# GpSimd copies the indices of a block of gathers two at a time, ahead of each pair, in a four-stage graph network on one core

## The chip, the cores and the metric

The program runs on one core of one Trainium2 chip. The metric is the device time of one execution in microseconds (us); lower is better. The engines are named as the profile names them: PE (TensorE), DVE (VectorE), ACT (ScalarE), POOL (GpSimd), and SP (SyncE), whose instructions are nearly all issues of transfers. "PEld" is PE's loading of weights. A "q" behind a name (SPq) is the engine's sequencer, which waits, computes registers and issues transfers.

## The reference

The graph has 6,250 nodes with 64 features and 200,000 edges sorted by their target. Four networks follow one another, each with a residual sum and a layer norm. The part around the change is the first one, two layers of graph attention with four heads:

```python
z = (x @ W).reshape(N, H, F)
el = jnp.sum(z * al, axis=-1)
er = jnp.sum(z * ar, axis=-1)
e = jax.nn.leaky_relu(el[src] + er[dst], 0.2)
m = jax.ops.segment_max(e, dst, num_segments=N)
ex = jnp.exp(e - m[dst])
s = jax.ops.segment_sum(ex, dst, num_segments=N)
alpha = ex / s[dst]
msg = z[src] * alpha[..., None]
out = jax.ops.segment_sum(msg, dst, num_segments=N) + b
```

What `el[src]` and `z[src]` ask for is one row of a table for each edge. The other three networks (a graph convolution of three layers, a plain sum over neighbours, and two convolutions with edge features) are sums over the same edges and come later in the program.

## The kernel before

**Blocks of gathers (POOL).** `table_d` in device memory holds, for each node, its features, a one and four logits (69 floats, 276 bytes). The 200,000 edges, padded to 98 x 2,048, are cut into 98 blocks. For a block, POOL issues 16 indirect DMAs (the gathers, L798), each of which brings 128 rows of the table into one of the three slots of a ring in SBUF; then it stores the slot to `msg_d` in device memory (L782), so that the rows lie there in the order of the edges. It does this for both attention layers (`blocks_pool`, called once for each), 196 blocks and 3,136 gathers in all. All indices of the core lie in `row_idx`; before the gathers of a block, POOL copies the block's 16 columns into `idx_cur` (L793) and waits on the semaphore `idx_here` for its own copy. The store of block j-1 is issued behind the third gather of block j (`store`), and behind the ninth POOL waits for that store to land and raises `msg_ready` (`ready`).

**Pace.** POOL doesn't gather as early as it can. DVE raises `dve_step` by eight for each group that it works through, in several portions. For each block a place was computed beforehand; ahead of the gathers k = 0, 2, 4, ... POOL waits until `dve_step` has reached that place plus k * 10 // 16. The first three blocks of the first layer have no place. The places are set so that a block is asked for 32 steps (four groups) ahead of the first group that reads it.

**Groups of windows.** A window is ten nodes and up to 384 edges, a group is five windows; there are 125 groups in each layer, five to a pass of a loop of 25. For a group, SP in program order:

- waits until DVE (and PE) are done with the slot, and loads the records of the next group's edges from `rec_d` (L498, five transfers) and, for two or three groups in five, their edge features (L500, five transfers);
- waits until `msg_ready` has reached the last block that the group needs, and until PE is done with the group of five groups ago (`win_psum`);
- loads `er_sl` (L516) and the five windows' rows from `msg_d` (L519).

DVE makes the one-hot matrices of three windows (first layer) or two (second layer) for the adjacency of the later networks (L1018, L1019), then works on the group's rows (first at L1041): logits, their maximum, the difference (L1045 to L1070, L1151). ACT scales one-hots (L1889), takes exponentials (L1949) and empties PE's banks; PE makes the adjacency products (L1610, L1612) and the weighted sums (L1631). SP can load a group's rows some groups before DVE works on them. After the second attention layer, the convolutions read the adjacency matrices back from device memory; POOL has no work there.

`wait_reg` (L354 to L356) is a wait on a register's value, which also raises a counter of its own.

Of the kernel before, what the change touches and what calls it, by code (L numbers as in the profile page):

```python
# [65 lines left out]
BK = 16  # L66
BLK = P * BK
NBLK = EP // BLK
# [5 lines left out]
PER_BLOCK = STEPS * NGR // NBLK  # L74
# [6 lines left out]
def build(nc, a):  # L81

    ctx = ExitStack()
    with ctx:
# [3 lines left out]
        def sem(name):  # L88
            return ctx.enter_context(nc.semaphore(name))
# [32 lines left out]
        def new(parts, *dims):  # L122
            off = top[0]
            top[0] += (int(np.prod(dims)) + 7) // 8 * 8
            return at(off, parts, *dims)
# [28 lines left out]
        row_idx = new(P, EC).bitcast(I32)  # L154
        idx_cur = new(P, RING, BK).bitcast(I32)
# [148 lines left out]
        def s(name):  # L304
            if name not in S:
                S[name] = sem(name)
            return S[name]
# [45 lines left out]
        def wait_reg(eng, semaphore, value):  # L353

            eng.wait_ge(semaphore, value)
            eng.sem_inc(s(f"passed_{'sp' if eng is nc.sync else 'pool'}"), 1)  # L356

        def rounds(eng, count, peel=True):

            if peel:  # L360
                yield 0
            with eng.Fori(int(peel), count) as i:
                yield i
# [8 lines left out]
        def range_from_one(eng, count):  # L372

            with eng.Fori(1, count) as i:
                yield i
# [39 lines left out]
        def first(b):  # L415
            return isinstance(b, int) and b == 0
# [358 lines left out]
        def blocks_pool(pool, layer):  # L775

            g_ = nc.gpsimd
            uses_before = [layer * len(range(i, NBLK, RING)) for i in range(RING)]

            def store(j, i, uses):  # L780
                wait_reg(pool, gathered[i], uses * (16 * BK) + 16 * BK)
                g_.dma_start(msg_d[bass.ds(j * BLK, BLK), :].rearrange("(p k) f -> p (k f)", k=BK), ring[:, i]).then_inc(msg_stored[i], 16)  # L782

            def ready(i, uses):
                wait_reg(pool, msg_stored[i], uses * 16 + 16)
                pool.sem_inc(s("msg_ready"), 1)

            def block(j, i, uses, former):
                if not isinstance(j, int) or j >= RING or layer:
                    place = pool.value_load(pace_row[0:1, layer, bass.ds(j, 1)], min_val=1, max_val=HEAD + 2 * NGR * STEPS + PER_BLOCK)  # L790
                else:
                    place = None
                g_.tensor_copy(idx_cur[:, i], row_idx[:, bass.ds(j * BK, BK)]).then_inc(s("idx_here"), 1)  # L793
                wait_reg(pool, s("idx_here"), j + (layer * NBLK + 1))
                for k in range(BK):
                    if place is not None and k % 2 == 0:
                        wait_reg(pool, s("dve_step"), place + k * PER_BLOCK // BK)
                    g_.indirect_dma_start(ring[:, i, k * XC:(k + 1) * XC], None, table_d, bass.IndirectOffsetOnAxis(  # L798
                        ap=idx_cur[:, i, k:k + 1], axis=0)).then_inc(gathered[i], 16)
                    if former is not None and k == BK // 8:  # L800
                        store(j - 1, (i - 1) % RING, former)
                    if former is not None and k == BK // 2:
                        ready((i - 1) % RING, former)

            def former_uses(it, i):
                return it + uses_before[(i - 1) % RING] - (1 if i == 0 else 0)

            pool.wait_ge(s("table_stored"), 16 * (layer + 1))
            if layer == 0:
                for i in range(RING):  # L810
                    block(i, i, 0, None if i == 0 else 0)
                pool.wait_ge(s("items_back"), 32)
            for it in (rounds(pool, NBLK // RING) if layer else range_from_one(pool, NBLK // RING)):
                for i in range(RING):
                    block(it * RING + i, i, it + uses_before[i], None if first(it) and i == 0 else former_uses(it, i))
            it = NBLK // RING
            for i in range(NBLK % RING):
                block(it * RING + i, i, it + uses_before[i], former_uses(it, i))
            last = NBLK - 1
            store(last, last % RING, last // RING + uses_before[last % RING])  # L820
            ready(last % RING, last // RING + uses_before[last % RING])
# [1292 lines left out]
```

## Time and profile before

| what | us |
|---|---|
| median of three runs (lowest, highest) | 7727.45 (7714.45, 7744.26) |
| the profiled execution, its own time | 7731.27 |
| span of the profile, first to last instruction | 7729.6 |
| POOL's first gather block to its last gather, first layer | 125.66 to 2753.6 |
| the same, second layer | 3027.59 to 5627.6 |
| busy: PE, DVE, ACT, POOL | 4457.3, 4150.8, 2129.1, 3270.2 |

The span is 1.7 us shorter than the profiled execution's own time. The program has three parts: the first attention layer up to about 2,860 us, the second up to about 5,860 us, the convolutions to the end. POOL works in the first two alone. Waits of SP are counted as SPq; its instructions are not counted as busy, so its load is read from how far apart its issues stand.

### The profile page before, as it was taken

Reading aid. Unit: us, or ns where it says so; the run is one execution under the profiler, and the core shown is the slowest. Engines: PE = TensorE matmul, PEld = TensorE weight load, DVE = VectorE, ACT = ScalarE, POOL = GpSimd, SP = SyncE. Lnnn points to the kernel's source line nnn. Section 1 sums busy time; section 2 is a strip of 40 time slices with the busy share of each in tenths; the row PEclk is TensorE's granted clock in tenths of the full one; section 3 lists DMA queues with packets and bytes.
Section 4 is the critical chain, followed back from the end, with each engine's and each line's share of the span. In section 5 each row is a group of like instructions: output and inputs, shape, how many; then the busy total and the mean of one; then the engine's idle time right before and its main releaser. Section 6 shows DMA issues by size and latency. Waiting matters only on the chain.

```text
span 7729.6 us, 118765 instructions
## 1 busy us (share of the span) xinstructions
PE 4457.3 (58%) x28553; PEld 2928.7 (38%) x28553; DVE 4150.8 (54%) x13273; ACT 2129.1 (28%) x5938; POOL 3270.2 (42%) x3549
## 2 busy tenths in 40 slices
PE   1455555555555565344444444444477988888865
PEld 1223333223233235122222222222256767676754
DVE  3566676767676663455655565556574111223344
ACT  0344444444444441133333233333320000000000
POOL 3666666656565612666666666656600000000000
PEclk9666766666776665566666666666667999999988
DMA  5454454545444532344444444444437989899976
GB/s 88 112 144 134 136 145 131 145 129 145 136 143 134 143 113 49 97 111 122 121 112 121 121 121 116 120 110 123 120 108 287 416 340 416 345 416 401 373 291 260
DMA packets 934339, 1390.68 MB, mean 180 GB/s; under 512 B 483496, under 2 KB 689474, under 8 KB 917769
## 3 DMA queue, kind: packets, MB, share of 16 engines
q1 hardware_dynamic: 687776, 912.42, 35.0%
q0 software_dynamic: 128976, 222.12, 11.6%
q10 hardware_dynamic: 117332, 253.47, 8.8%
q8 instruction: 71, 1.16, 0.1%
q14 instruction: 184, 1.51, 0.1%
HBM read 1014.16 MB, written 373.27 MB: 179 GB/s over the span
## 4 chain that ended last, share of the span: by engine, by line
issue 18%; SPq 16%; PE 14%; another core or an unknown queue 13%; DVE 13%; DMA 13%; ACT 7%; DVEq 4%; ACTq 2%
DMA arena<-adj_w_d 8%; ACT arena L1889 4%; DMA arena<-adj_c_d 4%; SPq L498 4%; SPq L519 4%; PE bank L1754 3%; PE bank L1755 2%; PE bank L1758 2%; SPq L485 2%; DVE arena L1018 2%; PE bank L1716 2%; SPq L500 2%; PE bank L1610 1%; DVE arena L1041 1%
## 5 line engine op out<-in xcount | busy, mean ns | idle before, releaser
L798 POOL DMA_INDIRECT arena<-table_d,arena x3136 | 3093.4, 986 | 1956.7 <-issue 974.0
L1610 PE MATMUL bank<-arena 128*128 128x500 f16 x3750 | 1351.9, 497 | 1312.4 <-issue 720.1
L1631 PE MATMUL bank<-arena 128*65 128x40 f32 x7500 | 649.0, 257 | 1053.8 <-ACT arena L1949 538.8
L1610 PEld LDWEIGHTS bank<-arena 128*128 128x128 f16 x3750 | 430.2, 122 | 2026.1 <-issue 1798.0
L1889 ACT ACTIVATE arena<-arena 128x128 f16<-128x128 f16 x3750 | 1126.6, 392 | 239.1 <-DVEq L1119 133.0
L1631 PEld LDWEIGHTS bank<-arena 128*65 128x65 f32 x7500 | 618.0, 171 | 1174.0 <-issue 611.6
L1754 PE MATMUL bank<-arena 125*128 125x250 f16 x3750 | 857.9, 274 | 156.2 <-DMA arena<-adj_w_d 132.9
L1018 DVE TENSOR_SCALAR arena<-arena 128x500 f16<-128x500 f16 x1875 | 681.7, 364 | 411.5 <-issue 207.2
L1755 PE MATMUL bank<-arena 125*128 125x250 f16 x3750 | 853.9, 273 | 0.0
L1612 PE MATMUL bank<-arena 128*128 128x500 f16 x1875 | 695.7, 474 | 203.6 <-issue 200.1
L1104 DVE SCALAR_TENSOR_TENSOR arena<-arena,bank 128x250 f16<-128x250 f16 x1250 | 455.8, 412 | 559.2 <-ACT arena L1913 297.8
L1910 ACT ACTIVATE arena<-bank 128x500 f16<-128x500 f32 x625 | 365.2, 584 | 1296.8 <-remote 641.3
L1932 ACT ACTIVATE arena<-bank 65x200 f32<-65x200 f32 x250 | 83.1, 333 | 1574.0 <-remote 1523.0
L1019 DVE TENSOR_SCALAR arena<-arena 128x128 f16<-128x128 f16 x1875 | 511.5, 273 | 0.0
L1758 PE MATMUL bank<-arena 125*128 125x250 f16 x3750 | 443.1, 274 | 98.0 <-DMA arena<-adj_c_d 91.9
L1041 DVE TENSOR_TENSOR arena<-arena 128x200 f32<-128x200 f32 x750 | 340.3, 509 | 273.0 <-DMA arena<-msg_d 183.3
L1754 PEld LDWEIGHTS bank<-arena 125*128 125x128 f16 x3750 | 366.9, 98 | 250.8 <-DMA arena<-adj_w_d 159.4
L1612 PEld LDWEIGHTS bank<-arena 128*128 128x128 f16 x1875 | 219.1, 117 | 601.8 <-issue 500.3
L1758 PEld LDWEIGHTS bank<-arena 125*128 125x128 f16 x3750 | 358.9, 98 | 160.6 <-DMA arena<-adj_c_d 102.1
L1755 PEld LDWEIGHTS bank<-arena 125*128 125x128 f16 x3750 | 363.7, 97 | 50.1
L1913 ACT ACTIVATE arena<-bank 128x500 f16<-128x500 f32 x625 | 364.0, 582 | 0.0
L1605 PE MATMUL bank<-arena 128*102 128x30 f32 x1250 | 198.9, 300 | 221.4 <-issue 150.5
(244 smaller groups left out, 4244.8 us busy)
## 6 DMA issues: line engine op xcount, KB each, us to landing
arena<-adj_w_d SPq DMA_DIRECT2D x720, 625.0 KB, 10.8
arena<-adj_c_d SPq DMA_DIRECT2D x345, 625.0 KB, 11.4
adj_w_d<-arena ACTq DMA_DIRECT2D x125, 1250.0 KB
arena<-msg_d SPq DMA_DIRECT2D x1250, 103.5 KB
msg_d<-arena POOLq DMA_DIRECT2D x196, 552.0 KB
adj_c_d<-arena ACTq DMA_DIRECT2D x125, 625.0 KB
arena<-table_d,arena POOLq DMA_INDIRECT x3136
arena<-in_edge_features SPq DMA_DIRECT2D x625, 51.0 KB
```

The source lines that it names most:

```text
L798: g_.indirect_dma_start(ring[:, i, k * XC:(k + 1) * XC], None, table_d, bass.IndirectOffsetOnAxis(ap=idx_cur[:, i, k:k + 1], axis=0)).then ...
L1018: v.tensor_scalar(col_oh[:, slot, c, :], iota_key, key, None, ALU.is_equal)
L1019: v.tensor_scalar(row_oh[:, slot, c, 2, :], iota_lo, rec[:, c * REC + 1:c * REC + 2], None, ALU.is_equal)
L1041: v.tensor_tensor(lg[:, 0:nw, c], bc(rows[:, :, c, F + 1:XC], 3, WN), e, ALU.add)
L1104: last = v.scalar_tensor_tensor(parts[:, h, 1], parts[:, h, 0], -LOW, whole[:, h], ALU.mult, ALU.add)
L1610: mm(wb, lhsT=row_oh[:, slot, c, i, :], rhs=col_oh[:, slot, c, :], start=(c == 0 and i == 0), stop=(c == CH - 1 and i == 1))
L1612: last = mm(cb, lhsT=row_oh[:, slot, c, 2, :], rhs=col_oh[:, slot, c, :], start=(c == 0), stop=(c == CH - 1))
L1631: last = mm(out, lhsT=rows_sl[:, g, w, c, 0:AGG], rhs=grh[:, g, w * CH + c, :], start=(c == 0), stop=(c == CH - 1))
L1754: mm(by_group(out), lhsT=x_one[:, tile, :], rhs=w_slots[slot][0:NT, :, 0, t, :], start=first_, stop=False)
L1755: return mm(by_group(out), lhsT=x_two[:, tile, :], rhs=w_slots[slot][0:NT, :, 1, t, :], start=False, stop=False)
L1758: return mm(by_group(out), lhsT=ones_of(n)[:, t, :], rhs=c_slots[slot][0:NT, :, t, :], start=t == 0, stop=stop)
L1889: last = act_(row_oh[:, slot, c, i, :], row_oh[:, slot, c, 2, :], ACT.Copy, scale=rec[:, c * REC + 2 + i:c * REC + 3 + i])
```

## The change

POOL's one copy of 16 columns for a block becomes eight copies of two columns, each ahead of the two gathers that use it. In front of each pair stand now, in this order: the wait on `dve_step`, the copy, the wait on `idx_here` for that copy. Before, the copy and its wait stood ahead of the first wait on `dve_step`.

```diff
-                g_.tensor_copy(idx_cur[:, i], row_idx[:, bass.ds(j * BK, BK)]).then_inc(s("idx_here"), 1)
-                wait_reg(pool, s("idx_here"), j + (layer * NBLK + 1))
                 for k in range(BK):
-                    if place is not None and k % 2 == 0:
-                        wait_reg(pool, s("dve_step"), place + k * PER_BLOCK // BK)
+                    if k % 2 == 0:
+                        if place is not None:
+                            wait_reg(pool, s("dve_step"), place + k * PER_BLOCK // BK)
+                        g_.tensor_copy(idx_cur[:, i, k:k + 2], row_idx[:, bass.ds(j * BK + k, 2)]).then_inc(s("idx_here"), 1)
+                        wait_reg(pool, s("idx_here"), j * (BK // 2) + (layer * NBLK * (BK // 2) + k // 2 + 1))
                     g_.indirect_dma_start(ring[:, i, k * XC:(k + 1) * XC], None, table_d, bass.IndirectOffsetOnAxis(
                         ap=idx_cur[:, i, k:k + 1], axis=0)).then_inc(gathered[i], 16)
```

## Rows read from the trace of the kernel before

**Rows 1.** Busy time by stretch: first layer, second layer, convolutions (200 us each).

```profile
core 0: us, PE busy (x) PEld busy (x) DVE busy (x) ACT busy (x) POOL busy (x), PEclk, DMA share, GB/s
1200.00:1400.00 200.00, 122.68 (x622) 65.27 (x620) 141.87 (x465) 93.33 (x265) 127.45 (x138) 0.68 0.50 142
4000.00:4200.00 200.00, 84.10 (x506) 49.63 (x507) 120.50 (x390) 65.69 (x184) 126.20 (x136) 0.63 0.45 121
6000.00:6200.00 200.00, 181.12 (x1585) 151.70 (x1584) 26.75 (x104) 14.38 (x39) 0.00 (x0) 0.99 1.02 416
```

**Rows 2.** What SP's queue waited for, 3250 to 5600 us: total, times, longest.

```profile
SPq L356 <- remote: 8.6, 1, 8.6
SPq L356 <- PE bank L1605: 0.7, 1, 0.7
```

**Rows 3.** The same view of DVE, second layer (3250 to 5600 us), first lines.

```profile
DVE arena L1104 <- ACT arena L1913: 226.9, 27, 17.5
DVE arena L1041 <- DMA arena<-msg_d: 152.8, 30, 13.2
```

**Rows 4.** The same view of POOL, 150 to 2750 us: its waits for DVE's steps.

```profile
POOL arena L798 <- DVEq L1032: 329.4, 99, 9.7
POOL arena L798 <- DVEq L1154: 93.4, 24, 7.7
POOL arena L798 <- DVEq L1136: 85.6, 49, 4.0
```

**Rows 5.** POOL's costliest groups, whole span: count | busy, mean ns.

```profile
L798 POOL DMA_INDIRECT arena<-table_d,arena x3136 | 3093.4, 986 | 1956.7 <-issue 974.0 <-DVEq L1032 747.6 <-DVEq L1154 105.2
L782 POOL DMA_DIRECT2D msg_d<-arena x196 | 116.5, 594 | 19.9 <-DMA arena<-table_d,arena 9.5 <-issue 7.6 <-DVEq L1136 2.4
L793 POOL COPY arena<-arena 128x16 int32 (+1 forms) x196 | 45.6, 232 | 354.8 <-DMA table_d<-arena 352.9 <-issue 0.9
```

**Rows 6.** POOL in order of time, a block in which it waits for nobody: start, us.

```profile
145.99 0.95 POOL L798 DMA_INDIRECT arena<-table_d,arena  x1 [0.30 <-issue]
146.94 0.21 POOL L793 COPY arena<-arena 128x16 int32<-128x16 int32 x1
147.93 0.97 POOL L798 DMA_INDIRECT arena<-table_d,arena  x1 [0.79 <-POOL arena L793]
149.21 0.94 POOL L798 DMA_INDIRECT arena<-table_d,arena  x1 [0.30 <-issue]
```

**Rows 7.** The copy of L793 by duration (ns min/median/max); POOL's smallest operation.

```profile
L793 POOL COPY arena<-arena x196: 195/208/837, 125.7 to 5605.8; 128x16 int32 x186, 128x16 int32<-128x16 int32 x10
L793 POOL COPY arena<-arena x96: 202/208/837, 172.3 to 2721.1; 128x16 int32 x93, 128x16 int32<-128x16 int32 x3
0.44 0.10 POOL L2085 MEMSET const-float32-1.0<- 128x1 f32 x1
```

**Rows 8.** End of each layer: POOL's last gather and store, SP's last group.

```profile
2752.68 0.95 POOL L798 DMA_INDIRECT arena<-table_d,arena  x1 [0.30 <-issue]
2755.88 0.58 POOL L782 DMA_DIRECT2D msg_d<-arena  x1 [2.25 <-DMA arena<-table_d,arena]
2777.38 0.34 SPq L516 DMA_DIRECT2D arena<-er_d  x1
...
5629.91 0.58 POOL L782 DMA_DIRECT2D msg_d<-arena  x1 [2.33 <-DMA arena<-table_d,arena]
5667.43 0.34 SPq L516 DMA_DIRECT2D arena<-er_d  x1
```

**Rows 9.** Start of the second layer: POOL, SP and DVE in order of time.

```profile
3027.59 0.20 POOL L793 COPY arena<-arena 128x16 int32<-128x16 int32 x1 [271.13 <-DMA table_d<-arena]
3048.75 0.21 POOL L793 COPY arena<-arena 128x16 int32<-128x16 int32 x1
3049.85 0.97 POOL L798 DMA_INDIRECT arena<-table_d,arena  x1 [0.88 <-issue]
...
3056.75 0.95 POOL L798 DMA_INDIRECT arena<-table_d,arena  x1 [0.30 <-issue]
3060.51 0.95 POOL L798 DMA_INDIRECT arena<-table_d,arena  x1 [0.30 <-issue]
3063.31 0.70 SPq L516 DMA_DIRECT2D arena<-er_d  x1
3083.56 1.34 DVE L1041 TENSOR_TENSOR arena<-arena 128x200 f32<-128x200 f32 x3 [28.11 <-issue]
```

**Rows 10.** A copy and a DVE operation that began together.

```profile
3455.23 0.83 POOL L793 COPY arena<-arena 128x16 int32 x1
...
3455.23 0.78 DVE L1151 TENSOR_TENSOR arena<-arena 128x600 f32<-128x600 f32 x1 [1.12 <-issue]
```

**Rows 11.** SP's issues of records with POOL gathering throughout, then with POOL waiting.

```profile
1337.20 0.01 SPq L498 DMA_DIRECT2D arena<-rec_d  x1
1339.34 0.71 SPq L500 DMA_DIRECT2D arena<-in_edge_features  x1
1341.47 0.01 SPq L498 DMA_DIRECT2D arena<-rec_d  x1
...
1335.06 0.95 POOL L798 DMA_INDIRECT arena<-table_d,arena  x1 [0.30 <-issue]
1336.31 0.95 POOL L798 DMA_INDIRECT arena<-table_d,arena  x1 [0.30 <-issue]
...
4111.24 0.33 SPq L500 DMA_DIRECT2D arena<-in_edge_features  x1
4111.76 0.33 SPq L498 DMA_DIRECT2D arena<-rec_d  x1
4112.27 0.33 SPq L500 DMA_DIRECT2D arena<-in_edge_features  x1
...
4116.45 0.98 POOL L798 DMA_INDIRECT arena<-table_d,arena  x1 [6.93 <-DVEq L1032]
```

## The prediction

> **What bounds the kernel now.** I read the busy time by stretch first. No engine is full in the two attention layers: DVE has the most, 142 us in 200 in the first layer and 120 in 200 in the second, POOL 127 and 126 [rows 1]. In the convolutions POOL has nothing, so the change can act only before about 5,700 us. Next come the waits. In the second layer SP, over 2,350 us, waited only 9.3 us, and never for POOL [rows 2], while DVE waited 153 us there for rows from `msg_d` [rows 3]. The reader should see two things: SP is the stage that runs without pause in the second layer, and POOL is never late for it. POOL's own waits are for DVE's steps, 508 us in the first layer [rows 4]: it is held back by its pace, not by its work. In the first layer DVE, ACT and PE hand work round, and SP is ahead of them.
>
> So POOL has spare time, and the question is how much, and whether the change spends it.
>
> **POOL's work for a block, before.** A gather takes 986 ns [rows 5] and the next starts 0.30 us later [rows 6]; 16 make 16 x 1.286 = 20.6 us. The store adds its 0.59 [rows 5]. The copy takes 0.23 [rows 5] and the gather behind it starts 0.79 us after its end when no step is waited for [rows 6], instead of 0.30; with the step's wait behind it that was 0.88 [rows 9]. I take 0.23 + 0.88 - 0.30 = 0.81. Together 22.0 us for a block with no wait.
>
> **POOL's work after.** Eight copies of two columns. How long is one? No row shows it. From above it is the copy of 16 columns, 0.208 median, 0.232 mean [rows 5, 7]; from below the smallest POOL operation, 0.10 us for 128x1 [rows 7]. A copy of 16 columns is so small already that I take it as nearly all fixed cost: 0.22, near the upper end. Then 0.79 to the gather; the new order has no other wait in between. The price of a pair is 0.22 + 0.79 - 0.30 = 0.71, of eight pairs 5.7. A gather behind a copy took 0.97 where the next took 0.94 [rows 6]: 7 x 0.025 = 0.2 more. The block is 20.6 + 0.6 + 5.7 + 0.2 = 27.0 us with no wait, 5.0 more than before; with copies of 0.10 it is 26.1, and with 0.1 us more for each pair, for registers of the new wait values, 27.8. These two are the bounds.
>
> **What POOL has.** In the first layer its copies go from 125.7 to 2721.1 [rows 7] over 97 blocks: 26.76 us a block; in the second from 3027.6 to 5605.8 [rows 7, 9]: 26.58. At the end it is early: the store starts at 2755.88, SP asks for it only just before 2777.38 [rows 8]. Take 3 us for the landing of the store, my estimate from the 2.25 us that the gather took to land [rows 8]: 18 us to spare; in the second layer 5667.4 - 5630.5 - 3 = 34. In mid-layer the code gives as much or more: a block is asked for 32 steps ahead, is through 10 steps later and stored some 5 after; the 17 left, at 8 steps a group and 26.76 x 98 / 125 = 21 us a group, are 45 us. If POOL never waited, it would have to be through by 2777.4 - 6 (its last gather's landing, its store, the store's landing) = 2771.4, that is 2645.7 / 98 = 27.0 us a block; in the second layer (5661.4 - 3027.6) / 98 = 26.9.
>
> So the new block of 27.0 us lies at the limit. The 508 us of waits are spent almost exactly by 98 x 5.0 = 490 us of new work, and the lead covers what is missing. In the first layer the loss is 0; in the second 98 x (27.0 - 26.9) = some 10 to 14 us.
>
> **The start of the second layer** has no cover. The first group needs block 0, announced behind the ninth gather of block 1. Before, POOL's sequencer was ahead of its engine and could announce it by about 3056.75, and SP asked just ahead of its issue at 3063.31 [rows 9]; I take 3061. After, the sequencer can't be more than a pair ahead: block 0 takes 25.6 us, then four pairs, a store and a fifth copy, 12.8 + 0.6 + 1.0: 3067.6. SP is about 7 us late, and DVE, which waits 28 us for these rows already [rows 9], with it. SP runs without pause in this layer, so it doesn't catch up; but the 10 to 14 us at the layer's end are measured against SP's old time, so of the two the larger counts: 14.
>
> **Copies against DVE.** A copy that began with a DVE operation on two SBUF operands took 0.83 instead of 0.21, and ended with it [rows 10]. Mean less median of the copies is 0.024 us, 12% [rows 5, 7]. If DVE loses as much for each copy as POOL, the 1,372 new ones cost it 33 us; at most the whole copy, 0.2 each, 274; at least nothing. DVE sets the pace in the first layer alone and there in part: I take 8.
>
> The Trainium skill ("SBUF — State Buffer", section "SBUF: two separate sides") calls this an exclusive lock, which whoever starts first holds for the whole instruction, against a DVE operation with two SBUF inputs or in a mode with two ports. The trace agrees for the copy's side. If every new copy held DVE up for its whole length, the sum would be 274 us more, less what DVE idles; it is the reason for the fourth case below.
>
> **Sum.** 7731.3 of the profiled execution, + 0 + 14 + 8 = 7753; the profiled execution lies 4 above the median, so 7750 against 7727.
>
> **The rivals.**
>
> *POOL becomes the bound.* Same mechanism, price a little higher. At 27.5 us a block, first layer 98 x 0.5 = 49, second 98 x 0.6 = 59, with the rest 7727 + 49 + 59 + 8 = 7843. It decides from about 27.2 us, only 0.03 us more for each pair than I take, which is why its chance is large. For it: POOL still waits for steps in places where these come late, and such waits can't be made up for when its work fills its time; a wait that binds now also has a copy behind it (0.22 + 0.79 + about 0.1, against 0.75 before). Against it: the lead of 45 us in mid-layer.
>
> *Faster: SP is relieved.* SP issues records 2.1 us apart while POOL gathers without a break, and 0.5 apart while POOL waits [rows 11]. The copies put about 1 us without a gather behind every second gather, and the waits of 7 to 10 us go. If SP runs faster when gathers are thinned out, the second layer, where SP has no slack [rows 2], gets shorter. What speaks against it: SP's slow and fast stretches only change places, the number of gathers stays, and POOL's own 27.0 us a block caps it. With the lower bound of 26.1 a block, the layer could be 98 x (26.9 - 26.1) = 78 us shorter: about 7660. It decides from 26.5 us a block down.
>
> The Trainium skill ("DMA: Bandwidth & Descriptors", section "SWDGE vs HWDGE vs iDMA") has SP's descriptors come from dedicated hardware with no software in the loop. By that, POOL's gathers would not slow SP's issues, and this rival would be worth 0; rows 11 disagree.
>
> *The new copies slow DVE* beyond what I take: with a third of the upper bound on its path, 90 us, 7727 + 14 + 90 = 7831. For it the coincidence in rows 10, against it a copy's median that stands only 13 ns above its minimum [rows 7].
>
> **How the numbers follow.** A measurement of this kernel can tell about 0.5%, 39 us, from no change. Forecast (POOL at its limit, 7700 to 7766) 0.43; POOL bound 0.35; SP relieved 0.14; DVE slowed 0.08. Faster 0.14, within 0.5% 0.43, slower 0.43. The upper end takes in 27.5 us a block and a little more, 7860; the lower end half of the gain of the relieved SP, 7690. The forecast's own range is 7710 to 7766.
>
> **What the profile of the changed kernel would show.** The copies' row: 1,568 of them at 0.19 to 0.23 us; if 0.10 to 0.12, the lower bound holds. The gather behind one starts 0.79 us after its end; 0.9 or more means POOL is the bound. POOL's waits for DVE's steps fall from about 500 us a layer to below 100. SP's waits in the second layer: none if I am right; if POOL is the bound, SP waits in front of L516. The last store of each layer comes within 10 us of SP's last L516, instead of 21 and 37. The first L1041 of the second layer has some 7 us more idle time ahead of it. SP's issues stand less far apart if the third case holds, and DVE's waits for `msg_d` shrink. What would make the prediction wrong: a pair's price off by more than 0.03 us, or an SP so much faster that the leads don't count.

## The result and the profile after

The changed kernel takes 7820.43 us (median of four runs, 7812.61 to 7826.34); the kernel before took 7726.89 on the same chip (four runs, 7714.45 to 7744.26). The ratio is 1.0119, 95% interval 1.0101 to 1.0137: slower by some 93 us, 1.2%. The profiled execution has a span of 7811.0 us against 7729.6. The time lies in the range given, but the forecast case (no change that can be measured, 7750) did not happen. It was the first rival: POOL became the bound. The range holds the measured time because its upper end had been set by that rival's 27.5 us a block; the sum itself, 7750, is 70 us short.

The page of the changed kernel: busy line, the first line of the chain that ended last, and three of the costliest groups.

```profile
PE 4416.8 (57%) x28553; PEld 2929.0 (37%) x28553; DVE 4132.0 (53%) x13273; ACT 2127.1 (27%) x5938; POOL 3621.4 (46%) x4921
...
issue 26%; POOL 20%; DMA 15%; DVE 14%; PE 12%; SPq 5%; DVEq 5%; POOLq 2%; ACT 0%; ACTq 0%
...
L799 POOL DMA_INDIRECT arena<-table_d,arena x3136 | 3143.7, 1002 | 1797.7 <-issue 1243.6
...
L1042 DVE TENSOR_TENSOR arena<-arena 128x200 f32<-128x200 f32 x750 | 338.4, 506 | 1403.9 <-DMA arena<-msg_d 1401.3
...
L797 POOL COPY arena<-arena 128x2 int32 (+1 forms) x1568 | 347.8, 222 | 301.7 <-DMA table_d<-arena 293.9
```

A busy share of 46% hides the bound: POOL is busy only in the two layers, and between its operations lies time in which it waits for its own copy or issues the next gather. The chain shows it better: POOL has 20% of it, and SP's queue 5%. In the kernel before, the same line has no POOL at all and SP's queue at 16%:

```profile
issue 18%; SPq 16%; PE 14%; another core or an unknown queue 13%; DVE 13%; DMA 13%; ACT 7%; DVEq 4%; ACTq 2%
```

("issue" can be idle time of any engine, so only a part of its 26% is POOL's.) The copies' row has the duration that was forecast, 0.222. The gathers' row does not: 1,002 ns where it was 986 [rows 5].

Busy time by stretch, the same stretches as [rows 1]:

```profile
1200.00:1400.00 200.00, 102.61 (x603) 56.10 (x603) 134.75 (x452) 87.67 (x250) 134.19 (x182) 0.74 0.50 140
4000.00:4200.00 200.00, 82.14 (x470) 45.32 (x469) 115.28 (x376) 60.86 (x171) 132.91 (x181) 0.64 0.44 113
```

DVE falls from 142 and 120.5 to 135 and 115: it gets its rows more slowly. Who is late is read from the waits. SP's waits, 3250 to 5600 us, which were 9.3 us and none for POOL [rows 2]:

```profile
SPq L356 <- POOLq L786: 1153.3, 85, 19.9
```

DVE's waits in the same stretch [rows 3]:

```profile
DVE arena L1042 <- DMA arena<-msg_d: 751.3, 64, 16.1
```

POOL's waits, 150 to 2750 us [rows 4]:

```profile
POOL arena L799 <- POOL arena L797: 215.6, 273, 0.8
POOL arena L799 <- DVEq L1137: 5.2, 17, 0.3
POOL arena L799 <- DVEq L1033: 3.4, 11, 0.3
POOL arena L799 <- DVEq L1155: 3.3, 11, 0.3
```

POOL's waits for DVE's steps went from 508 us to 12: its spare time is spent. SP, which had waited for nobody, now stands half of the stretch in front of POOL's announcement (L786), and DVE stands 751 us instead of 153 for rows from `msg_d`.

POOL in order of time, in mid-layer, and a place where the gather behind a copy starts late:

```profile
641.58 0.26 POOL L797 COPY arena<-arena 128x2 int32 x1
644.31 0.97 POOL L799 DMA_INDIRECT arena<-table_d,arena  x1 [2.48 <-issue]
...
4022.44 0.19 POOL L797 COPY arena<-arena 128x2 int32 x1
4023.41 0.97 POOL L799 DMA_INDIRECT arena<-table_d,arena  x1 [0.79 <-issue]
4024.69 0.95 POOL L799 DMA_INDIRECT arena<-table_d,arena  x1 [0.30 <-issue]
```

A pair is 0.19 + 0.79 + 0.97 + 0.30 + 0.95 = 3.2 us. The ends of the two layers and the start of the second, for [rows 8] and [rows 9]:

```profile
2827.43 0.95 POOL L799 DMA_INDIRECT arena<-table_d,arena  x1 [0.30 <-issue]
2831.34 0.58 POOL L782 DMA_DIRECT2D msg_d<-arena  x1 [2.96 <-DMA arena<-table_d,arena]
2835.30 0.34 SPq L516 DMA_DIRECT2D arena<-er_d  x1
3043.70 0.18 POOL L797 COPY arena<-arena 128x2 int32<-128x2 int32 x1 [211.78 <-DMA table_d<-arena]
3085.64 0.34 SPq L516 DMA_DIRECT2D arena<-er_d  x1
3091.20 1.34 DVE L1042 TENSOR_TENSOR arena<-arena 128x200 f32<-128x200 f32 x3 [25.50 <-DMA arena<-msg_d]
5755.48 0.95 POOL L799 DMA_INDIRECT arena<-table_d,arena  x1 [0.30 <-issue]
5759.10 0.68 POOL L782 DMA_DIRECT2D msg_d<-arena  x1 [2.68 <-DMA arena<-table_d,arena]
5762.58 0.34 SPq L516 DMA_DIRECT2D arena<-er_d  x1
```

From these rows the 81.4 us between the two spans (7811.0 - 7729.6) can be laid out:

- POOL begins the second layer 16.1 us later (3043.70 against 3027.59).
- From there to SP's last L516 it takes 2718.9 us instead of 2639.8: 79.1.
- From there to the end it takes 13.8 less (7811.0 - 5762.58 = 2048.4 against 7729.6 - 5667.43 = 2062.2).

The ends of the layers are odd. SP's last group in the first layer came 58 us later than before (2835.30 against 2777.38), yet the second layer started only 16 us later; and the part behind the second layer's last group got shorter. DVE's first operation on the last group of each layer explains both; before, then changed kernel:

```profile
2840.45 1.35 DVE L1041 TENSOR_TENSOR arena<-arena 128x200 f32<-128x200 f32 x3
5696.10 1.35 DVE L1041 TENSOR_TENSOR arena<-arena 128x200 f32<-128x200 f32 x3
2856.10 1.36 DVE L1042 TENSOR_TENSOR arena<-arena 128x200 f32<-128x200 f32 x3
5778.06 1.36 DVE L1042 TENSOR_TENSOR arena<-arena 128x200 f32<-128x200 f32 x3
```

SP had been 63.1 us ahead of DVE at the end of the first layer and is now 20.8 ahead: 42 of the 58 us took up its lead and cost nothing, and DVE came 15.7 us later. At the end of the second layer the lead went from 28.7 to 15.5 us, so of SP's 95.2 us DVE felt 82.0. That is nearly the whole difference of the spans.

SP and POOL together at the end of the first layer, changed kernel:

```profile
2822.49 0.33 SPq L500 DMA_DIRECT2D arena<-in_edge_features  x1
2822.89 0.97 POOL L799 DMA_INDIRECT arena<-table_d,arena  x1 [0.79 <-POOL arena L797]
2823.01 0.33 SPq L498 DMA_DIRECT2D arena<-rec_d  x1
2823.52 0.33 SPq L500 DMA_DIRECT2D arena<-in_edge_features  x1
2824.17 0.95 POOL L799 DMA_INDIRECT arena<-table_d,arena  x1 [0.31 <-issue]
2824.56 0.33 SPq L500 DMA_DIRECT2D arena<-in_edge_features  x1
```

SP issues mostly 0.52 us apart while POOL gathers, where in [rows 11] it issued 2.1 us apart under gathers without a break. So the second rival's mechanism is there as well: SP is relieved. Its gain can't be had while POOL sets the pace. I summed it over the trace: between group 6 and group 121 of a layer, the time less what SP stood idle in front of its semaphore instructions, divided by 115 groups. SP's active time a group was 19.0 us in the first layer and 20.3 in the second; it is 11.9 and 11.1 now. It isn't only the issues that were slow. Of SP's register instructions (MOVE and FUSED_REGOPS, which issue nothing) from 3250 to 5000 us, 19% lasted over 0.5 us before and 0.4% do in the changed kernel, while a typical MOVE takes 0.03 us in both.

### The profile page after: what moved, and what is told of

Same layout as the page of the kernel before. It is cut to its first block, busy times and chain, and to the rows that moved or that the text cites. A ratio compares the mean times of both kernels' runs of the same rounds, so it can differ in the third digit from the quotient of the medians.

```text
span 7811.0 us, 124113 instructions
## 1 busy us (share of the span) xinstructions
PE 4416.8 (57%) x28553; PEld 2929.0 (37%) x28553; DVE 4132.0 (53%) x13273; ACT 2127.1 (27%) x5938; POOL 3621.4 (46%) x4921
## 4 chain that ended last, share of the span: by engine, by line
issue 26%; POOL 20%; DMA 15%; DVE 14%; PE 12%; SPq 5%; DVEq 5%; POOLq 2%; ACT 0%; ACTq 0%
POOL arena L799 17%; DMA arena<-adj_w_d 8%; DMA arena<-adj_c_d 4%; POOL arena L797 3%; PE bank L1755 3%; DMA arena<-msg_d 2%; PE bank L1756 2%; PE bank L1759 2%; PE bank L1717 2%; DVE arena L1019 2%; SPq L519 2%; DVEq L1033 2%; DVE arena L1042 1%; SPq L485 1%; DVE arena L1049 1%
## 5 line engine op out<-in xcount | busy, mean ns | idle before, releaser
L799 POOL DMA_INDIRECT arena<-table_d,arena x3136 | 3143.7, 1002 | 1797.7 <-issue 1243.6
L1611 PEld LDWEIGHTS bank<-arena 128*128 128x128 f16 x3750 | 444.8, 128 | 2833.4 <-issue 2458.7
L1632 PE MATMUL bank<-arena 128*65 128x40 f32 x7500 | 593.2, 252 | 286.4 <-ACT arena L1950 207.9
L1632 PEld LDWEIGHTS bank<-arena 128*65 128x65 f32 x7500 | 572.9, 163 | 418.8 <-ACT arena L1950 277.4
L1950 ACT ACTIVATE arena<-arena 128x600 f32<-128x600 f32 x250 | 175.7, 703 | 1948.9 <-DVEq L1154 1112.6
L1911 ACT ACTIVATE arena<-bank 128x500 f16<-128x500 f32 x625 | 362.4, 580 | 1115.1 <-PE bank L1613 797.1
L1020 DVE TENSOR_SCALAR arena<-arena 128x128 f16<-128x128 f16 x1875 | 489.0, 261 | 0.0
L797 POOL COPY arena<-arena 128x2 int32 (+1 forms) x1568 | 347.8, 222 | 301.7 <-DMA table_d<-arena 293.9
L1606 PEld LDWEIGHTS bank<-arena 128*102 128x102 f32 x1250 | 204.5, 263 | 514.6 <-issue 431.0
## 6 DMA issues: line engine op xcount, KB each, us to landing
arena<-adj_c_d SPq DMA_DIRECT2D x345, 625.0 KB, 11.4
```

Of the source, the lines that this page charges most:

```text
L797: g_.tensor_copy(idx_cur[:, i, k:k + 2], row_idx[:, bass.ds(j * BK + k, 2)]).then_inc(s("idx_here"), 1)
L1020: v.tensor_scalar(row_oh[:, slot, c, 2, :], iota_lo, rec[:, c * REC + 1:c * REC + 2], None, ALU.is_equal)
L1611: mm(wb, lhsT=row_oh[:, slot, c, i, :], rhs=col_oh[:, slot, c, :], start=(c == 0 and i == 0), stop=(c == CH - 1 and i == 1))
L1632: last = mm(out, lhsT=rows_sl[:, g, w, c, 0:AGG], rhs=grh[:, g, w * CH + c, :], start=(c == 0), stop=(c == CH - 1))
```

## The experiments

The theory after the result has two parts. **Price:** each pair costs POOL a copy and a wait of 0.79 us behind it, and a block of some 27.6 us is more than POOL has. **Relief:** a gap after every second gather makes SP faster, and this is worth much wherever POOL isn't the bound. The rivals: the copies themselves cost (their number, or their port); SP isn't relieved by the gap but by POOL's held sequencer; each layer pays alike. Where an expectation names a theory by a letter, A is price, B the copies themselves, C the held sequencer as a cost to POOL, D and G relief by the gap, and H the held sequencer as the relief of SP.

All ratios are to the kernel before on the same chip. It took 7795.32 (runs 1 to 4), 7805.14 (5 to 8) and 7784.47 us (9 to 12) on the three chips of the runs, against 7726.89 on the chip of the result; the changed kernel itself ran only there. So ratios are compared between chips and not times, except where POOL sets the pace, as said there. The kernel before has no trace on those chips either. One layer each of runs 9 and 10 is its code: the sum of SP's active time gives 20.9 us a group there in the second layer and 20.5 in the first, a little more than on the first chip.

**Run 1, the eight copies together at the head of the block, one wait.**

```diff
+for k in range(0, BK, 2):
+    g_.tensor_copy(idx_cur[:, i, k:k + 2], row_idx[:, bass.ds(j * BK + k, 2)]).then_inc(s("idx_here"), 1)
+wait_reg(pool, s("idx_here"), j * (BK // 2) + (layer * NBLK * (BK // 2) + BK // 2))
 for k in range(BK):
     ...
-        g_.tensor_copy(idx_cur[:, i, k:k + 2], ...)
-        wait_reg(pool, s("idx_here"), ...)
```

> Eight copies of two columns as in the changed kernel, but all at the start of the block, with one wait for the eighth. Theory A (the changed kernel is bound by POOL's time for a block, and that time comes from the wait of 0.79 us behind each copy): a block without waits takes about 22.0 + 7 x 0.22 = 23.5 us, under the 26.6 to 26.8 that the rest asks for, so the time is that of the kernel before, 7727 within 30. Theory B (the copies themselves slow DVE through the shared access to SBUF): as many copies as in the changed kernel, so about 7820.

Measured: 7734.41 us, ratio 0.9911 (0.989 to 0.9933). The same 1,568 copies of two columns, and no loss. (That it is 0.9% faster than the kernel before, no theory had said.) SP's issues in this kernel:

```profile
4046.05 0.01 SPq L498 DMA_DIRECT2D arena<-rec_d  x1
4048.20 0.69 SPq L500 DMA_DIRECT2D arena<-in_edge_features  x1
4050.34 0.02 SPq L498 DMA_DIRECT2D arena<-rec_d  x1
4051.78 0.70 SPq L500 DMA_DIRECT2D arena<-in_edge_features  x1
```

They stand 1.4 to 2.1 us apart again, and SP's active time is back at 20.2 and 20.6 us a group. Neither the number of copies nor their port costs the time; the place of the waits does.

**Run 2, each pair's copy issued one pair ahead,** so that its wait is over when it is reached.

```diff
+        if k == 0:
+            copy(0)
+        if k + 2 < BK:
+            copy(k + 2)
         wait_reg(pool, s("idx_here"), j * (BK // 2) + (layer * NBLK * (BK // 2) + k // 2 + 1))
```

> Eight copies, each issued one pair ahead of the gathers that use it, so that the wait for it is over when it is reached; only the first pair of a block waits. Theory A: the idle time of 0.79 us behind a copy goes back to 0.30 or less, a block takes about 23.8 us, and the time is 7727 within 30. Theory B: about 7820. Theory C (what costs is that POOL's sequencer is held at a wait by each pair, so that it can't run ahead): it is no longer held, so as theory A; if the gather behind a copy starts late even though the wait is over, the block stays near 27 and the time near 7820.

Measured: 7700.64 us, ratio 0.9871 (0.985 to 0.9892). SP's active time 18.9 and 20.5. Copies spread over the block but without the wait behind them cost nothing, and relieve SP little. Where the 1.3% come from isn't shown.

**Run 3, four copies of four columns, each with its wait; run 4, two of eight.** The waits on `dve_step` stay at every pair.

```diff
+    if k % 4 == 0:
+        g_.tensor_copy(idx_cur[:, i, k:k + 4], row_idx[:, bass.ds(j * BK + k, 4)]).then_inc(s("idx_here"), 1)
+        wait_reg(pool, s("idx_here"), j * (BK // 4) + (layer * NBLK * (BK // 4) + k // 4 + 1))
```

> Four copies of four columns, each ahead of four gathers, with its wait; the waits for DVE's steps stay at every pair. Theory A: a block without waits takes 22.0 + 3 x 0.71 = 24.1 us, so POOL is not the bound: 7727 plus at most 7 for the start of the second layer. Theory D (SP's slow stretches come from POOL's long runs of gathers, and a gap of 1 us breaks them): SP's slow instructions get rarer than before and the second layer gets shorter, since POOL can now do it in 2,400 us: 7600 to 7700.

> Two copies of eight columns, each ahead of eight gathers. Theory A: a block takes 22.7 us, time 7727 within 15. Theory D: a smaller part of the gain of the version with four copies.

Measured: four copies 7320.15 us, ratio 0.9376 (0.9351 to 0.9401); two copies 7800.75 us, ratio 0.9998 (0.9984 to 1.0013). With four, the costliest wait of SP (first line of its view, 3250 to 5200 us) and POOL in order of time:

```profile
SPq L356 <- POOLq L786: 86.6, 17, 10.3
```

```profile
4112.93 0.19 POOL L798 COPY arena<-arena 128x4 int32 x1
4113.91 0.97 POOL L800 DMA_INDIRECT arena<-table_d,arena  x1 [0.79 <-issue]
4115.18 1.04 POOL L800 DMA_INDIRECT arena<-table_d,arena  x1 [0.30 <-issue]
```

The reader should see that the copy and its wait are the same as in pairs, 0.19 and 0.79. There are half as many of them, so POOL's block takes 24.5 us in the second layer and SP hardly waits for it. SP's active time is 18.8 and 17.2 us a group. This kernel is 6% faster than the one before: the same edit as the change at half the rate. Price alone had it at 7727 or a little more, relief at 7600 to 7700; it is some 300 us below that, so relief is worth far more than I had thought. With two copies nothing of the gain that relief forecast is there.

**Run 5, a fill in place of the copy.** One copy of sixteen a block as before, and between pairs a fill of 128x640 that nothing waits for at once (only for the fill one pair earlier).

```diff
+        if k:
+            wait_reg(pool, s("idx_here"), j * (BK // 2) + (layer * NBLK * (BK // 2) + k // 2))
+            g_.memset(scratch, 0.0).then_inc(s("idx_here"), 1)
```

> The kernel before (one copy of 16 columns), and ahead of each further pair of gathers a memset of 128x640 on POOL, which nobody waits for at once (each waits only for the memset of the pair before, long done). So gathers come in pairs with about 0.93 us between pairs, as in the changed kernel, but POOL's sequencer isn't held until its engine has run dry. Theory G (SP is relieved by a gap of about 1 us between gathers): SP waits for POOL in both layers, as in the changed kernel, SP's issues stand close together, and the time is that of a block of 26.7 us, 7730 to 7830. Theory H (SP is relieved when POOL's sequencer is held until its gathers are issued): SP is as slow as in the kernel before, hardly waits for POOL, and DVE waits for msg_d as before.

Measured: 7496.41 us, ratio 0.9605 (0.9574 to 0.9636). POOL in order of time, and SP's first wait, 3250 to 5600 us:

```profile
4028.87 0.66 POOL L802 MEMSET arena<- 128x640 f32 x1
4029.69 0.96 POOL L803 DMA_INDIRECT arena<-table_d,arena  x1 [0.17 <-POOL arena L802]
```

```profile
SPq L357 <- POOLq L787: 688.3, 62, 17.6
```

The gap between gathers is 0.66 + 0.17 = 0.83 us without a held sequencer, and SP's active time is 13.1 and 12.0 us a group. So the relief comes with a gap that is filled by other work too. Two readings are left: the sequencer still is never more than a pair ahead here, and gathers might simply be rarer. Run 11 has the same waits and no relief, which speaks against the first. Against the second: the kernel before gathers more seldom (a block in 26.5 us of the second layer, on the average) and SP is slow in it. So it is how the gathers are spaced, not how many there are.

POOL still is the bound (26.0 us a block, SP waits 688 us for it), but at a lower price. I had forecast 26.7 a block and 7730 to 7830, and missed by the gap's length. POOL's block explains the time: 98 x 2 x (27.6 - 26.0) = 314 us less than the changed kernel's 7820 would be 7506. The fill has a price of its own, on DVE. The group of DVE's 128x500 operations in this kernel and in the changed kernel:

```profile
L1024 DVE TENSOR_SCALAR arena<-arena 128x500 f16<-128x500 f16 x1875 | 885.4, 472 | 131.0 <-issue 116.3
```

```profile
L1019 DVE TENSOR_SCALAR arena<-arena 128x500 f16<-128x500 f16 x1875 | 677.7, 361 | 131.0 <-issue 114.9
```

1,372 fills of 0.67 us lengthen this operation from 361 to 472 ns; 1,568 copies of 0.22 us left it at 361 (364 before, with 196 copies). The Trainium skill ("SBUF — State Buffer", section "SBUF: two separate sides") describes an exclusive lock between GpSimd and a VectorE operation that needs the shared pair of ports; the fills agree with it, and the copies show that small operations are not felt here.

**Run 6, a fill of 128x1 with a wait behind it ahead of each further pair; run 7, ahead of each further four.** One copy of sixteen a block.

```diff
+    if k and k % 2 == 0:        # run 7: k % 4
+        g_.memset(scratch, 0.0).then_inc(s("idx_here"), 1)
         wait_reg(pool, s("idx_here"), j * (BK // 2) + (layer * NBLK * (BK // 2) + k // 2 + 1))
```

> The kernel before (one copy of 16 columns), and ahead of each further pair a memset of 128x8 on POOL with a wait for it, in place of the changed kernel's copy. Theory A (the wait of 0.79 us, not the copying, is the price): the memset takes about 0.11 instead of 0.22, so a block takes 0.8 us less than in the changed kernel, and the time is about 98 x 2 x 0.8 less, less what the first layer hides: 70 to 150 below the changed kernel. Theory B (the copies' reads of SBUF slow DVE): DVE's own work gets shorter and the time falls below the kernel before.

> As the version with four copies of four columns, but with one copy of 16 and three memsets of 128x8 with their waits. If the halt and not the copy relieves SP, the time is that of the version with four copies or, as a block takes 0.4 us less and POOL is close to the bound there, up to 60 us below it.

The kernels that ran fill 128x1, not the 128x8 of the expectations. Measured: pairs 7676.52 us, ratio 0.9831 (0.98 to 0.9862); fours 7460.84 us, ratio 0.9564 (0.9528 to 0.9599). The gap in run 6:

```profile
4043.78 0.11 POOL L801 MEMSET arena<- 128x1 f32 x1
4044.68 0.94 POOL L803 DMA_INDIRECT arena<-table_d,arena  x1 [0.79 <-POOL arena L801]
```

The wait behind the smallest operation is the same 0.79. The gap is 0.90, the block 26.9 us, and SP still waits 1,077 us for POOL: pairs keep POOL the bound. No copy of indices is needed to get all that pairs do to SP (active 12.0 and 11.3). The time is 144 us below the changed kernel's 7820, and 98 x 2 x (27.6 - 26.9) gives 137: where POOL sets the pace, times agree between chips. It also lies below the kernel before, the sign that had been named for B, but DVE's 128x500 operation takes 363 ns against 361, so DVE's own work didn't get shorter. The comparison holds because the kernel before, which SP paces, is 78 us slower on this chip. Run 7 was forecast at run 3's time or below; it is 141 us above it.

**Run 8, one gather in four.** It leaves three quarters of the gathers out (the ring holds ones there), so its output isn't the reference's; it tells what the rest of the kernel needs.

```diff
-    g_.indirect_dma_start(ring[:, i, k * XC:(k + 1) * XC], ...)
+    if k % 4 == 0:
+        g_.indirect_dma_start(ring[:, i, k * XC:(k + 1) * XC], ...)
```

> The kernel before with one gather in four: the other twelve 128-row pieces of a block are left at 1.0, so its output is not the reference's; stores, announcements and paces stay. Shows what the rest needs when POOL gathers little. Theory D (POOL's gathers slow SP, and SP sets the second layer's pace): SP's issues stand 0.5 us apart nearly everywhere and both layers get 2 to 4 us a group shorter: 6,800 to 7,300. If POOL's gathers don't slow SP: within 50 us of the kernel before.

Measured: 6371.8 us, ratio 0.8161 (0.8136 to 0.8187), below the 6,800 to 7,300 expected. Busy time by stretch:

```profile
1200.00:1400.00 200.00, 118.05 (x703) 64.02 (x703) 161.29 (x549) 104.20 (x296) 42.28 (x53) 0.74 0.52 150
4000.00:4200.00 200.00, 129.29 (x762) 71.19 (x763) 166.18 (x547) 93.49 (x260) 50.18 (x64) 0.70 0.53 151
```

DVE gets up to 161 and 166 us in 200, and SP's active time is 11.4 and 11.1 us a group: about the level that pairs bring it to. Gathers and what they do to SP cost the kernel before about 1,430 us (7805 - 6372); the two parts of that aren't separated by this run.

**Runs 9 and 10, pairs in one layer alone,** the copy of sixteen in the other.

```diff
+pairs = layer == 0             # run 10: layer == 1
+if not pairs:
+    g_.tensor_copy(idx_cur[:, i], row_idx[:, bass.ds(j * BK, BK)]).then_inc(s("idx_here"), 1)
```

> The changed kernel in the first layer, the kernel before in the second. In the changed kernel GpSimd ended layer 0 late (SyncE's last group 58 us later), but GpSimd began layer 1 only 16 us later, since SyncE had run three groups ahead of VectorE. If that slack is the reason, this costs 16 us and little else: ratio 1.001 to 1.004. Rival (each layer pays alike): half of the 93 us, ratio 1.006. GpSimd 27.6 us a block in layer 0 and 26.5 in layer 1.

> The kernel before in the first layer, the changed kernel in the second, whose end is the end of the kernel. If GpSimd's blocks are the bound there, it costs (27.7 - 26.5) x 98 less what of it the lead takes up, by the two traces some 65 to 80 us: ratio 1.008 to 1.010. Rival (each layer pays alike): 1.006. The two costs of this pair of runs should add up to 1.012.

Measured: pairs in the first layer 7793.71 us, ratio 1.0009 (0.9996 to 1.0023); in the second 7805.2 us, ratio 1.0037 (1.002 to 1.0054). The copies of the paired layer in run 10:

```profile
L803 POOL COPY arena<-arena x784: 182/196/842, 3043.7 to 5749.2; 128x2 int32 x186, 128x2 int32<-128x2 int32 x10
```

From the first copy to the last, with some 3 us for the last pair, that is (5749.2 - 3043.7 + 3) / 98 = 27.6 us a block, as in the changed kernel (3043.7 to 5753.2). The first layer alone can't be told from no change, as the lead of SP has it and against "each layer alike" (1.006). The second was forecast at 1.008 to 1.010 and missed; it is below "each alike" too, and the sum of the two is 1.0046, not 1.0119.

The traces of these two runs show why, since each has the other's layer as the kernel before has it. From POOL's start in the second layer to DVE's first operation on its last group takes 2730.5 us with pairs (run 10) and 2716.3 with the code before (run 9); on the chip of the result it was 2734.4 and 2668.5. So pairs take as long on both chips, because POOL sets their pace, and the code before, which SP paces, is 48 us slower on this one. The loss of 1.2% belongs to the chip of the result; that the difference comes from the chip and not from something else that day isn't shown. Elsewhere the changed kernel wasn't run; if it takes its 7820 us there too, as POOL's pace would have it, it is some 0.2 to 0.5% slower than the kernel before, an estimate from 7784 to 7805 us.

**Run 11, a fill of 128x320 between pairs; run 12, a fill of 128x640 between fours.**

```diff
-scratch = new(P, 640)
+scratch = new(P, 320)          # run 12: 640, and the fill and its wait only where k % 4 == 0
```

> One copy of sixteen indices a block, and ahead of each further pair a fill of 128x320 in place of 128x640, not waited for at once: GpSimd's gap between pairs falls from 0.93 us to some 0.6, and its block unwaited from 25.9 us to some 24.5. If SyncE is relieved by each gap, whatever its length, GpSimd still sets the pace: 24.6 a block, some 7200 us, ratio 0.93. If the relief grows with the length of the gap, SyncE or VectorE sets it: over 25 a block, SyncE's active time a group above 15 us, ratio 0.95 to 0.97.

> As the fill of 128x640 between pairs, but ahead of every fourth gather alone: three gaps of 0.93 us a block, GpSimd's block unwaited some 24.1 us. If gaps are what SyncE needs and three of 0.9 us do as much as the three of 1.0 us in the kernel with four copies of four indices, the time is that kernel's: ratio 0.935 to 0.945. If it is the held sequencer of GpSimd at the wait behind its own copy that gives SyncE its room, SyncE is slowed more than there: ratio above 0.955.

Measured: run 11 7523.85 us, ratio 0.9677 (0.9648 to 0.9706); run 12 7584.51 us, ratio 0.9753 (0.9726 to 0.978). The gap in run 11 is 0.38 + 0.17 = 0.55 us:

```profile
4024.91 0.38 POOL L802 MEMSET arena<- 128x320 f32 x1
4025.46 0.95 POOL L803 DMA_INDIRECT arena<-table_d,arena  x1 [0.17 <-issue]
```

At 0.55 us SP's active time is 18.1 and 19.2 us a group where at 0.83 it was 13.1 and 12.0: the relief depends on the gap's length (the second of the two cases in the expectation), and POOL, with a shorter block, no longer is the bound. I had 0.93 us for the gap of run 5 in the expectations; these rows give 0.83.

What all runs say together (gap: end of one gather to the start of the next where something stands between; active: SP's, as summed above, second layer):

| run | a gap after every | gap us | SP active | us a group, second layer | ratio |
|---|---|---|---|---|---|
| changed kernel | 2 | 0.98 | 11.1 | 21.7 | 1.0119 |
| 6 | 2 | 0.90 | 11.3 | 21.1 | 0.9831 |
| 5 | 2 | 0.83 | 12.0 | 20.4 | 0.9605 |
| 11 | 2 | 0.55 | 19.2 | 20.3 | 0.9677 |
| 3 | 4 | 0.98 | 17.2 | 19.3 | 0.9376 |
| 7 | 4 | 0.90 | 18.8 | 19.9 | 0.9564 |
| 12 | 4 | 0.82 | 19.1 | 20.2 | 0.9753 |
| 4 | 8 | 1.0 | 19.8 | 20.9 | 0.9998 |
| 1 | 16 | 1.9 | 20.6 | 21.3 | 0.9911 |
| 2 | 2 | 0.34 | 20.5 | 21.0 | 0.9871 |

In the first three rows POOL is the bound: a longer gap is slower. In the fours SP hardly waits for POOL, and a longer gap is faster; but these three ran on three chips, and differ in more than the gap. The best of all is where neither waits long for the other.

Three things stay open. What it is in a gather that slows SP's instructions, no run shows. Run 12 differs from run 3 not only by its gap: nothing holds POOL's sequencer in it, and its fills slow DVE (404 ns for the 128x500 operation). So the second reading that I wrote down for run 12, that the held sequencer is needed, fits its 0.9753 as well; against it stand runs 5 and 11 alone. And run 4, with a gap of the full length after every eighth gather, gained nothing while run 1, with one after sixteen, gained 0.9%; I have no reason for that.

## Why the prediction came out as it did

**POOL's block.** This is the term of the sum that failed, by little: 27.0 us forecast. The last gather ends, less the first copy, give (2828.4 - 126.1) / 98 = 27.6 in the first layer and (5756.4 - 3043.7) / 98 = 27.7 in the second. The copy (0.22) and the wait (0.79) were right. What was missing:

- The gathers take 1,002 ns instead of 986: 16 x 0.016 = 0.26 us a block. I had allowed 0.2 of it, for the gathers behind a copy; 0.06 is left.
- At every 32nd copy, four blocks apart, 47 times in all, the gather starts 2.48 us behind the copy instead of 0.79 (at 641.58, and likewise at 420.7, 531.6 and 752.8): 1.69 / 4 = 0.42 us a block. No row of before shows it; there POOL's sequencer was several gathers ahead, and I take it that this covered it. Run 6 has the same 47 stalls without the copies, and run 5, where the sequencer is a pair ahead, has none.

27.0 + 0.06 + 0.42 = 27.5. The last 0.1 or 0.2 is spread over copies and waits that are a little longer on the average than in the rows. The prediction said that POOL as the bound decides from 27.2, 0.03 us a pair above the value taken. The value it rested on was added up mostly from single rows in which nothing disturbed POOL; a bound is reached by the mean with all its stalls.

**What POOL has.** 27.0 and 26.9 us a block were right as the limit before SP waits: with 27.7 the second layer should cost 98 x 0.8 = 78, and its part measured 79.1. For the first layer the rival had 49 us. SP's last group came 58 us later, but only 16 us reached the second layer. I read SP's own last issue as the layer's end and didn't ask how far it was ahead of DVE.

**The rival's time.** 7843 forecast, 7820 measured. Its 49 + 59 + 8 became 16 + 79 - 14: the second layer was dearer, the first cheaper, and the rest of SP's lead, 13 us, gave something back. That 7843 is only 23 us off is in part luck: its parts are wrong by 20 to 33 us each, in both directions.

**The start of the second layer.** I had SP about 7 us late for the first group. Counted from POOL's start, its wait ended 8.2 us later, and its L516 was issued 6.2 later (3085.64 - 3043.70 against 3063.31 - 3027.59). But DVE began on the rows 47.5 us after POOL's start instead of 56.0 (3091.20 - 3043.70 against 3083.56 - 3027.59), 8.5 earlier; SP issued their loads faster. The step was right and its consequence wrong: DVE's idle time there is 25.5 us instead of 28.1, not 7 more.

**Copies against DVE.** I took 8 us of at most 274. Run 1 with the same copies is not slower, and the 128x500 operation is as short as before. The term is 0, and the fourth case is ruled out.

**SP relieved.** I gave it 0.14, with the remark that POOL's 27.0 us a block caps it. Both halves are shown: SP's active time fell by 45% in the second layer, and nothing came of it while POOL set the pace. What I set against it, that SP's slow and fast stretches only change places, is wrong. The active time isn't conserved; it depends on how the gathers are spaced. The Trainium skill ("DMA: Bandwidth & Descriptors", section "SWDGE vs HWDGE vs iDMA") has no software in SP's descriptor path; by that I had argued that gathers would be nothing to SP, and runs 3, 5 and 11 differ from it by 3 to 6% of the whole time. The two needn't contradict each other: the page speaks of descriptors, and what slowed here were SP's instructions, register moves among them.

**The signs.** Most came true: copies of 0.22 us, waits for DVE's steps of 12 us, SP waiting for POOL if POOL is the bound, the last stores 4.0 and 3.5 us ahead of SP's last L516. One didn't: 0.9 us or more behind a copy was to show that POOL is the bound. It is the bound at 0.79, since the loss came from the number of waits and the stalls, not from a longer wait.

## What to carry to other kernels

Before a wait is put on an engine's own last operation, count how often it stands: here 0.79 us each, invisible once per sixteen gathers and the bound once per two. When a forecast of an engine's work comes within 3% of what it has, treat it as the bound, and look for stalls that its run-ahead hides today. And look at what the engines next to it do during the gap: a pause of 1 us after every fourth gather made this kernel 6% faster, since the stage that really set the pace was slowed by unbroken gathers.

## What the runs showed of the hardware

- SP's own instructions slow down while POOL gathers back to back: issues 2.1 us apart instead of 0.52, and 19% of its register instructions over 0.5 us instead of 0.4%. A gap of 0.83 to 0.98 us after every second gather takes this away almost wholly (active time 20.3 to 11 or 12 us a group); one of 0.55 us does nearly nothing (19.2). With one gather in four it is 11.1.
- A gather behind a POOL operation that it waits for starts 0.79 us after it, whether that is a copy of 128x2, of 128x4 or a fill of 128x1; behind a fill that it doesn't wait for, 0.17. Behind the eight copies of run 1 it was 0.90.
- A copy of 128x2 took 0.19 us, a fill of 128x1 0.11, one of 128x320 0.38 and one of 128x640 0.66.
- Every 32nd copy (64 gathers and four stores apart) the next gather is 1.69 us later, if POOL's sequencer waits for each pair (changed kernel and run 6, 47 times each); with a sequencer one pair ahead (run 5) it isn't seen. What happens there isn't shown.
- Fills of 0.67 us between pairs lengthened DVE's 128x500 operation from 361 to 472 ns; copies of 0.22 us left it as it was.
- The kernel before, which SP paces, took 7727 us in the runs of the result and 7784, 7795 and 7805 on the three chips of the later ones. The second layer with pairs, which POOL paces, took 2734 us in the first and 2731 in run 10.
